# Three fp32r terms for the routed experts' down projection of a fused attention and mixture-of-experts block

## What is computed

```python
def _mlp(x, gw, uw, dw):
    return jax.nn.silu(x @ gw.T) * (x @ uw.T) @ dw.T
...
topk_idx, topk_w = _route(x2d, router_weight, e_score_correction_bias)   # 2 of 8 experts
cw = zeros((T, E)).at[arange(T)[:, None], topk_idx].add(topk_w)
routed, _ = scan(acc + cwe[:, None] * _mlp(x2d, gw, uw, dw))             # over the 8 experts
x = x + attention(xn) + routed + shared_mlp(xn)
```

## Time and profile before

| | us |
|---|---|
| median of 3 runs | 1184.96 |
| profiled execution, its own time | 1182.23 |
| its span | 1180.5 |
| from the third to the last but two down projection (34 steps of one tile) | 255.84 |

### The profile page before, as it was taken

The page is one execution under the profiler, slowest core; times in us unless marked ns, Lnnn a source line. Parts: engine busy times, 40 slices in busy tenths (PEclk is TensorE's granted clock), DMA queues, the critical chain, the costliest instruction groups (busy, mean ns, idle before and its releaser), DMA issues. The chain is left out here.

```text
span 1180.5 us, 19294 instructions
## 1 busy us (share of the span) xinstructions
PE 1064.8 (90%) x5379; PEld 816.7 (69%) x5380; DVE 780.8 (66%) x1729; ACT 647.6 (55%) x1291; POOL 508.1 (43%) x567
## 2 busy tenths in 40 slices
PE   6979995888999999989999999978988999999994
PEld 4838883666677776767777777756766777777773
DVE  6822324556678868777777787645466777778772
ACT  4532220455777767777777777752154555555551
POOL 0008305289656555556556555651002333333331
PEclk9999995889899999999999999998989999999998
DMA  6969549978255264344345535018895443333342
GB/s 206 311 267 371 205 193 198 142 117 144 44 144 144 50 193 109 121 124 127 94 116 144 144 78 183 2 37 276 259 342 140 72 71 63 68 70 69 71 72 36
DMA packets 104648, 165.70 MB, mean 140 GB/s; under 512 B 49040, under 2 KB 59600, under 8 KB 101360
## 3 DMA queue, kind: packets, MB, share of 16 engines
q1 hardware_dynamic: 94128, 143.88, 42.8%
q0 software_dynamic: 9856, 20.53, 9.8%
q10 hardware_dynamic: 576, 0.26, 0.1%
HBM read 103.35 MB, written 61.28 MB: 139 GB/s over the span
## 5 line engine op out<-in xcount | busy, mean ns | idle before, releaser
L1160 POOL TENSOR_TENSOR prob_lo<-prob,prob_hi 128x512 fp32r<-128x512 f32 (+2 forms) x320 | 308.8, 978 | 239.6 <-ACT prob_hi L1209 223.9
L1202 ACT ACTIVATE prob<-ps_s 128x512 f32<-128x512 f32 (+3 forms) x384 | 188.2, 490 | 150.2 <-PE ps_s L1421 104.0
L1209 ACT ACTIVATE prob_hi<-prob 128x512 fp32r<-128x512 f32 (+3 forms) x384 | 198.5, 517 | 12.8 <-ACT row_stage L1183 12.7
L1272 DVE CUSTOM_DVE_ANT_0 ps_m<-ps_m,causal 128x384 f32<-128x384 f32 (+3 forms) x256 | 126.0, 498 | 69.8 <-PE ps_m L1392 68.9
L1828 DVE TENSOR_TENSOR rw_lo<-gu_sb,rw_hi 128x704 fp32r<-128x704 f32 x156 | 138.8, 893 | 47.9 <-ACT rw_hi L1763 42.2
L1742 POOL DMA_INDIRECT out<-work,rows x39 | 61.7, 1582 | 243.4 <-DVE rows L1789 118.0
L1392 PE MATMUL ps_m<-ks,qs 96*128 96x512 f32 (+3 forms) x384 | 143.7, 376 | 22.6 <-DMA ks<-qk_hi 13.6
L1439 PE MATMUL ps_o<-prob_hi,vs 128*66 128x512 f32 (+3 forms) x384 | 133.9, 349 | 18.8 <-issue 11.5
L1763 ACT ACTIVATE rw_hi<-gu_sb 128x704 fp32r x156 | 123.3, 792 | 46.6 <-PE ps_ru L1861 31.6
L1416 PE MATMUL ps_s<-qs,ks 97*128 97x512 f32 (+3 forms) x384 | 138.7, 361 | 2.4 <-ACT prob L1202 2.3
L1441 PE MATMUL ps_o<-prob_lo,vs 128*66 128x512 f32 (+3 forms) x384 | 131.1, 342 | 0.0
(11 more groups left out here) (212 smaller groups left out, 2422.4 us busy)
## 6 DMA issues: line engine op xcount, KB each, us to landing
xt<-xt_blocks SPq DMA_DIRECT2D x8, 2048.0 KB, 9.2
v_rows<-work SPq DMA_DIRECT2D x16, 512.0 KB, 2.9
qk_hi<-work SPq DMA_DIRECT2D x8, 1024.0 KB, 4.5
qk_lo<-work SPq DMA_DIRECT2D x8, 1024.0 KB, 7.1
qs<-qk_hi SPq DMA_DIRECT2D x64, 128.0 KB, 2.9
ks<-qk_hi SPq DMA_DIRECT2D x64, 128.0 KB, 3.1
vs<-v_rows SPq DMA_DIRECT2D x32, 256.0 KB, 4.8
out<-y_acc SPq DMA_DIRECT2D x32, 256.0 KB, 3.5
```

The costliest lines, as they stand in the source:

```text
L1160: nc.gpsimd.tensor_tensor(prob_lo[:, s % NPL, 0:w], prob[:, s % NP, 0:w], prob_hi[:, s % NPH, 0:w].bitcast(F32), ALU.subtract).then_inc(lo ...
L1202: nc.scalar.activation(prob[:, s % NP, 0:w], ps_s[s % NS][:, 0:w], ACT.Exp, scale=SCALE).then_inc(exp_done, 1)
L1209: nc.scalar.activation(prob_hi[:, s % NPH, 0:w], prob[:, s % NP, 0:w], ACT.Copy).then_inc(hi_ready, 1)
L1272: nc.vector.tensor_tensor_reduce(ps_m[s % NM][:, 0:w], ps_m[s % NM][:, 0:w], causal[:, TBW - w:], 1.0, MASKED, ALU.add, ALU.max, maxima[:, ...
```

## The change

The down projection of the routed experts is made in three fp32r terms too: nine matmuls of 512 columns for each tile instead of six fp32 passes. For it

- ACT rounds the turned units to `hid_t_hi` (two pieces) and the three chunks of down weights to `rd_hi`, for every tile. This stands at the front of its step, ahead of turning the next rows; `hid_t_hi` and `rd_hi` exist once, so that ACT waits for the down projection of the tile before (`y_done`, `d_used`).
- POOL subtracts the first two chunks (`rd_lo`, 128x512), between its gather and its scatter of a step.
- DVE subtracts the third chunk (96x512) and the units; the latter replace its two copies.
- ACT waits for the output projection's stores ahead of its first tile, since `rd_lo` lies where `y_tile` was.

Elsewhere several semaphores are merged into one; the instructions and their order stay. The core of the diff:

```diff
+        d_hi = nc.alloc_sbuf_tensor_at("rd_hi", [P, NF, D], F32R, offset=free)
+        d_lo = nc.alloc_sbuf_tensor_at("rd_lo", [P, NF, D], F32R, offset=y_at)
...
@@ block.gpsimd
-                pipeline(pool, NST, U, [(0, gather), (3, scatter)])
+                def down_lo(i, c):
+                    j = U * i + c
+                    e = expert(pool, j)
+                    for k in range(NF - 1):
+                        wait(pool, d_hi_ready, NF * j + k + 1)
+                        nc.gpsimd.tensor_tensor(d_lo[:, k, :], down_chunk(e, k),
+                                                d_hi[:, k, :].bitcast(F32),
+                                                ALU.subtract).then_inc(d_lo_ready, 1)
+
+                pipeline(pool, NST, U, [(0, gather), (2, down_lo), (3, scatter)])
...
@@ block.scalar
-                pipeline(act, NST, U, [(0, turn_x), (0, first_chunks), (1, gate_unit), (0, last_chunk)],
-                         back=R)
+                def turn_h(i, c):
+                    j = U * i + c
+                    w = FCH[-1][1]
+                    wait(act, h_turned, j + 1)
+                    wait(act, y_done, j)
+                    nc.scalar.activation(hid_t_hi[:, 0:2, :], ps_h[:, 0:2, :],
+                                         ACT.Copy).then_inc(h_hi_ready, 1)
+                    nc.scalar.activation(hid_t_hi[0:w, 2, :], ps_h[0:w, 2, :],
+                                         ACT.Copy).then_inc(h_hi_ready, 1)
+
+                def down_hi(i, c):
+                    j = U * i + c
+                    e = expert(act, j)
+                    act.wait_ge(experts_ready, e + 1)
+                    for k, (f0, w) in enumerate(FCH):
+                        if k < NF - 1:
+                            wait(act, d_used, (NF - 1) * (j - 1) + k + 1)
+                        else:
+                            wait(act, y_done, j)
+                        nc.scalar.activation(d_hi[0:w, k, :], down_chunk(e, k),
+                                             ACT.Copy).then_inc(d_hi_ready, 1)
+
+                for n in range(YS):
+                    act.wait_ge(y_stored[n], 16 * (NT // YS))
+                pipeline(act, NST, U, [(2, turn_h), (2, down_hi), (0, turn_x), (0, first_chunks),
+                                       (1, gate_unit), (0, last_chunk)], back=R)
...
@@ block.vector, turn_h and a new stage
-                    nc.vector.tensor_copy(hid_t[:, c % HR, 0:2, :], ps_h[:, 0:2, :]).then_inc(h_ready, 1)
...
+                    wait(dve, h_hi_ready, 2 * (j + 1))
+                    for rows_of, ks in ((P, slice(0, 2)), (w, slice(2, 3))):
+                        nc.vector.tensor_tensor(hid_t_lo[0:rows_of, ks, :], ps_h[0:rows_of, ks, :],
+                                                hid_t_hi[0:rows_of, ks, :].bitcast(F32),
+                                                ALU.subtract).then_inc(h_lo_ready, 1)
+
+                def last_down_lo(i, c):
...
+                    wait(dve, d_hi_ready, NF * (j + 1))
+                    nc.vector.tensor_tensor(d_lo[0:w, NF - 1, :], down_chunk(e, NF - 1),
+                                            d_hi[0:w, NF - 1, :].bitcast(F32),
+                                            ALU.subtract).then_inc(d_last_ready, 1)
...
-                pipeline(dve, NST, U, [(0, row_numbers), (4, turn_h), (2, x_lo), (2, first_chunks),
-                                       (3, hidden), (2, last_chunk), (4, weigh)], back=U)
+                pipeline(dve, NST, U, [(0, row_numbers), (4, turn_h), (4, last_down_lo), (2, x_lo),
+                                       (2, first_chunks), (3, hidden), (2, last_chunk),
+                                       (4, weigh)], back=U)
...
@@ block.tensor, down
-                        last = nc.tensor.matmul(
-                            ps_y[c % 2][:, :], hid_t[0:w, c % HR, k, :],
-                            d_sb[0:w, bass.ds(e * NF + k, 1), :].rearrange("p a d -> p (a d)"),
-                            start=(k == 0), stop=(k == NF - 1))
-                    last.then_inc(y_done, 1)
+                        if k < NF - 1:
+                            wait(pe, d_lo_ready, (NF - 1) * j + k + 1)
+                        else:
+                            wait(pe, d_last_ready, j + 1)
+                        for a, b in ((hid_t_hi, d_hi), (hid_t_hi, d_lo), (hid_t_lo, d_hi)):
+                            last = nc.tensor.matmul(ps_y[c % 2][:, :], a[0:w, k, :], b[0:w, k, :],
+                                                    start=(k == 0 and a is hid_t_hi and b is d_hi),
+                                                    stop=(k == NF - 1 and a is hid_t_lo))
+                        if k == NF - 1:
+                            last.then_inc(y_done, 1)
+                        else:
+                            last.then_inc(d_used, 1)
```

More of the change, by code:

```diff
@@ L147, in moe_attention_kernel @@
                 nc.sbuf_tensor("y_tile", [P, YS, D], F32) as y_tile:
+            y_at = nc.sbuf_base - YS * D * 4
             out_phase(nc, wo, gate, up, down, ident, work, gu_sb, d_sb, out, y_tile, y_stored,
                       slot_table, rows, rows_ready, xn_dram, gathered, passed, expert_loaded)
-            routed_phase(nc, gate, up, down, ident, gu_sb, d_sb, slot_table, expert_of, xn_dram,
+            routed_phase(nc, work_at, y_at, gate, up, down, ident, gu_sb, d_sb, slot_table, expert_of, xn_dram,
                          work, out, y_stored, rows, rows_ready, gathered, passed, expert_loaded,
@@ L374, in _ @@
                 act.wait_ge(r_loaded, 16)
-                nc.scalar.activation(r_hi[:, :, :], r_raw[:, :, :], ACT.Copy).then_inc(r_hi_ready, 1)
+                nc.scalar.activation(r_hi[:, :, :], r_raw[:, :, :], ACT.Copy).then_inc(wv_hi_ready, 1)
             @block.tensor
@@ L1659, in _, with routed_phase @@
                 pipeline(pe, NT, U, [(0, turn), (1, multiply)])
-def routed_phase(nc, gate, up, down, ident, gu_sb, d_sb, slot_table, expert_of, xn_dram, work, out,
+def routed_phase(nc, work_at, y_at, gate, up, down, ident, gu_sb, d_sb, slot_table, expert_of, xn_dram, work, out,
                  y_stored, rows, rows_ready, gathered, passed, expert_loaded, experts_ready):
@@ L1678, in routed_phase @@
         HR = 2
-        units = work[:, 3 * R:4 * R, :].rearrange("p a d -> p (a d)")
-        silu, hid = [units[:, n * HR * F:(n + 1) * HR * F].rearrange("p (u f) -> p u f", u=HR)
+        free = work_at + 2 * R * D * 4
+        hid_t_hi, hid_t_lo = [
+            nc.alloc_sbuf_tensor_at(f"hid_t{n}", [P, NF, P], F32R, offset=free + n * NF * P * 4)
+            for n in range(2)]
+        free += 2 * NF * P * 4
+        d_hi = nc.alloc_sbuf_tensor_at("rd_hi", [P, NF, D], F32R, offset=free)
+        d_lo = nc.alloc_sbuf_tensor_at("rd_lo", [P, NF, D], F32R, offset=y_at)
+        free += NF * D * 4
+        silu, hid = [nc.alloc_sbuf_tensor_at(f"units{n}", [P, HR, F], F32, offset=free + n * HR * F * 4)
                      for n in range(2)]
-        hid_t = work[:, 2 * R:2 * R + HR, 0:NF * P].rearrange("p u (k t) -> p u k t", k=NF)
+        assert free + 2 * HR * F * 4 <= work_at + NT * D * 4
         w_hi = sbuf("rw_hi", [P, KC, 2 * F], F32R)
@@ L1698, in routed_phase @@
         h_turned = sem("h_turned")
-        h_ready = sem("h_ready")
+        h_hi_ready = sem("h_hi_ready")
+        h_lo_ready = sem("h_lo_ready")
+        d_hi_ready = sem("rd_hi_ready")
+        d_lo_ready = sem("rd_lo_ready")
+        d_last_ready = sem("rd_last_ready")
+        d_used = sem("rd_used")
         y_done = sem("ry_done")
@@ L1801, in turn_h @@
                     j = U * i + c
-                    wait(dve, h_turned, j + 1)
-                    wait(dve, y_done, j - HR + 1)
-                    nc.vector.tensor_copy(hid_t[:, c % HR, 0:2, :], ps_h[:, 0:2, :]).then_inc(h_ready, 1)
                     w = FCH[-1][1]
-                    nc.vector.tensor_copy(hid_t[0:w, c % HR, 2, :], ps_h[0:w, 2, :]).then_inc(h_ready, 1)
+                    wait(dve, h_hi_ready, 2 * (j + 1))
[4 more added lines that the diff above has]
+                def last_down_lo(i, c):
+                    j = U * i + c
+                    e = expert(dve, j)
+                    w = FCH[-1][1]
+                    wait(dve, d_hi_ready, NF * (j + 1))
+                    nc.vector.tensor_tensor(d_lo[0:w, NF - 1, :], down_chunk(e, NF - 1),
+                                            d_hi[0:w, NF - 1, :].bitcast(F32),
+                                            ALU.subtract).then_inc(d_last_ready, 1)
                 def weigh(i, c):
@@ L1869, in turn_h @@
                     wait(pe, hid_ready, j + 1)
-                    wait(pe, h_ready, 2 * j)
+                    wait(pe, h_lo_ready, 2 * j)
                     for k, (f0, w) in enumerate(FCH):
@@ L1876, in down @@
                     j = U * i + c
-                    e = expert(pe, j)
-                    pe.wait_ge(experts_ready, e + 1)
-                    wait(pe, h_ready, 2 * (j + 1))
```

(8 more changed lines are left out.)

51 lines of the change are left out of this document (23 added, 28 removed).

## The result

| kernel | median of runs, us | ratio to before | 95% interval |
|---|---|---|---|
| before | 1184.08 | | |
| changed | 1285.56 (1280.76 to 1286.91) | 1.0845 | 1.0808 to 1.0883 |

The row "before" is now the median of four runs (1182.68 to 1187.52). The change makes the kernel slower by 101 us. I had said slower, but by 63 us, with 1274 as the upper end. The profiled execution took 1280.76 us with a span of 1279.1. Its page, to be read against the earlier trace rows: busy us of each engine with share and instructions, then the granted clock of PE in tenths over 40 slices.

The account below looks back on a forecast made before the run. Loop A was taken as the bound, 7.52 us a tile, rising to 9.2. 60.5 us over 18 loops + 2 head + 3 tail = 65.5 on 1182.23, so 1248; range 1214 to 1274.

Parts of the forecast that it names:

- rival 4: Routed phase: PE's clock falls in half of the steps, doubling turning rows and gate and up; +82 us, 1330; chance 0.04.
- loop A: Two-tile loop weighing, scatter, gather, turning rows, down projection: 15.04 us before, forecast 17.85, or 18.4 with port meetings.
- PE's work: Routed tile on PE: nine matmuls 0.23 us apart replace six fp32 passes; work falls by 0.5 us to 6.7.
- The port: SBUF port: DVE's third chunk delays POOL's second subtraction by 0.4 to 0.7 us, 0.2 to 0.35 a tile.
- loop B: One-tile loop: units turned, ACT's copies and roundings, DVE's third chunk, xg_lo, rw_lo, product of units; 8.6 or 9.75 us.
- Head and tail: Outside the tile loop: ACT's first rounding waits for stores, 2 us (0 to 3); last scatter and down projections, +3.
- The first: Rival: POOL wins the port, so loop B decides at 9.75 us a tile: 1267; chance 0.15.
- The second: Rival: loop A is shorter than counted, so loop B's 8.5 us is the limit: 1222; chance 0.16.
- The third: Rival: POOL's subtractions end before the weighing, outside loop A; only PE's 0.5 us a loop is left: 1175; chance 0.05.

Follow-up runs that it names:

- the filler: Changed kernel plus three useless fp32 matmuls of 352 columns per tile on PE, placed where it waits: 1246.45 us, ratio 1.0560.
- The run with MEMSETs: Changed kernel with four memsets in place of POOL's two subtractions, low parts of two chunks left out: 1279.62 us, ratio 1.0865.
- the gather-first run: Changed kernel with POOL's gather issued ahead of its subtractions and scatter: 1209.82 us, ratio 1.0227.

## Why the prediction was wrong in its size

**The step that failed** is in rival 4: "I expect PE to wait some 1.7 us a step". I had divided a pair's waiting evenly over its two steps. It isn't: one tile of a pair passes in 8.0 us without a wait for rows, and the other gets all of it, 1.21 + 3.45 us with 0.55 of work between. Then the granted clock falls, and 2.0 us of a pair are added to loop A itself, since turning rows and gate and up lie in it. The forecast itself had put this term at nothing. As a rival I had given it 0.04 and 82 us: it came in half of the steps, as supposed there, but turning rows and gate and up did not double, they grew from 4.3 to 6.26, since the clock was back before they ended. It took 39 us (by the filler) or 36 (by the windows).

The trace of the kernel before held the warning. The one wait of 3.4 us stands there at 887.5 to 890.90, and gate and up behind it take 5.49 us at 0.69, nearly to the digit what every second step does after the change:

```profile
891.31:896.80 5.49, 5.49 (x27) 5.49 (x26) 2.48 (x3) 2.84 (x4) 2.05 (x2) 0.69 0.73 180
```

My rival 4 set the routed phase's 0.99, "with waits up to 3.4 us", against itself. But in 282 us a single fall hardly moves the mean: I should have asked for the clock right behind the wait.

**What held.** The direction, and the loop that decides. With the useless matmuls the pair is 18.45 where I had taken 18.4, and the time 1246 where I had said 1248. But errors of both signs cancel in it, and that is luck. Between scatter and gather it was 0.47 more, since the scatter took 2.06 instead of 1.58 us, and to the weighing 0.35 more, since DVE finishes its last `rw_lo` first. To the scatter it was 0.6 to 0.9 less than the 5.3 to 5.6 that I had with the port (1.0 to 1.3 less in the pair with the filler): the units are turned and copied earlier than I had it, the port costs less, and the gap behind the subtractions is 0.16 and not 0.30. (15.30 a pair before is no error of 15.04: that is the mean of tiles 2 to 36, and the first pair, with the long wait, took 19.57.)

**PE's work.** Nine matmuls 0.23 us apart, as read in the earlier trace rows. **ACT** is busy for 6.1 us a tile (215.57 over 35.2 steps); 7.1 was forecast, of which 0.35 were a wait for issue. Part of the rest is overlap: three `rd_hi` take 1.68 together and not 3 × 0.63. **DVE** 6.8, forecast 6.6 to 7.0; its third chunk takes 0.81 in the median, above 0.69 as said. **POOL** 5.7 against 5.4.

**The port.** The two subtractions take 3.00 together and not 2 × 1.33, since DVE's third chunk goes between them. That is 0.34 each time, where I had forecast 0.4 to 0.7 (0.2 to 0.35 a tile, as loop A passes them once in two tiles). The Trainium skill ("SBUF — State Buffer", section "SBUF: two separate sides") says that the holder of the shared pair keeps it for the whole instruction; the 3.01 us of `rw_lo` beside 2.55 of subtractions agree. The run with MEMSETs shows that this hardly matters to the pair in the order that the change has, and the gather-first run that it costs 0.6 us a step where loop B decides.

**Head and tail.** ACT's first rounding starts 1.2 us after PE has turned the rows (858.30 against 857.07), forecast 2. The phase itself began 4 us earlier in this execution, so tile 0 is nevertheless weighed 0.8 earlier; counted from the first turned rows it is 3.3 later. The tail adds 3.3, forecast 3.

**Rivals.** The first (POOL always wins the port) did not come: the short steps are 8.0. The second, loop B at 8.5, is what the gather-first version runs into: 8.25. The third needed POOL's work outside loop A; even there, 1209.82, loop B keeps it slower than before.

## What to carry to other kernels

Where a loop runs over two steps, don't divide the wait by the number of steps: ask which step gets it, and whether the wait is then long enough for TensorE's clock to fall; if it is, the slower matmuls belong in the same loop. Look at what stands ahead of a gather in its engine's queue before adding anything there: two subtractions and their waits, on an engine that was busy 36% of the time, cost 8%, and moving the gather ahead gained 0.9% with no other change. Useless matmuls in the wait are a cheap test of a clock theory, as long as they leave TensorE some room.
